# Split products for the shared experts, and four summed rows a token, in a 64-expert layer

## What is computed

```
logits = flat @ router_w.T
_, topk_idx = top_k(logits + router_bias, 4)
topk_w = softmax(logits)[topk_idx], divided by its sum
slot = number of the token among those of its expert (first 64 kept)
y = einsum(silu(xg @ gate_w) * (xg @ up_w), down_w)        (for each expert)
out = zeros.at[tok_table].add(y * w_table)
sg = einsum('nd,sfd->nsf', flat, sh_gate_w)                (s: 2 shared experts)
su = einsum('nd,sfd->nsf', flat, sh_up_w)
out = out + einsum('nsf,sdf->nd', silu(sg) * su, sh_down_w)
x = layernorm(x + out)
```

## Time and profile before

| | |
|---|---|
| time, median of 3 runs | 2373.93 us (2370.86 to 2379.55) |
| profiled execution | 2381.64 us |
| its span | 2379.9 us |
| PE busy, of the span | 2139.5 us (90%) |
| DVE, ACT, POOL busy | 1362.7, 806.4, 674.3 us |
| shared products in stage C (two recorded matmuls each) | 768 matmuls, 344.5 us busy |

### The profile page before, as it was taken

How to read it: one execution, slowest core, us unless ns; L and a number is a source line. 1 busy time by engine, 2 the same in 40 slices (tenths; PEclk the granted TensorE clock), 3 DMA queues, 4 the chain that set the end, 5 groups by cost and what they waited for, 6 DMA issues and landing times. The chain is left out here.

```text
span 2379.9 us, 31463 instructions
## 1 busy us (share of the span) xinstructions
PE 2139.5 (90%) x10918; PEld 1180.7 (50%) x10919; DVE 1362.7 (57%) x3185; ACT 806.4 (34%) x1333; POOL 674.3 (28%) x945
## 2 busy tenths in 40 slices
PE   9999979979999999879999988578888888889994
PEld 5777748755444443445555543233333333336763
DVE  5866768846121226566777774845656565445443
ACT  5554624420112211333444433533322232123333
POOL 1200015516433321223343433011113131214553
PEclk9999989979999999998999997789999999999997
DMA  7211232270177764363333330200000000065555
GB/s 268 75 36 54 89 121 82 94 290 1 28 240 248 244 210 152 100 134 81 81 88 82 88 68 1 97 3 1 2 19 2 19 28 19 19 177 159 100 99 171
DMA packets 101178, 230.31 MB, mean 97 GB/s; under 512 B 18886, under 2 KB 42626, under 8 KB 93870
## 3 DMA queue, kind: packets, MB, share of 16 engines
q1 hardware_dynamic: 78478, 186.61, 25.3%
q0 software_dynamic: 22560, 41.87, 7.9%
HBM read 169.45 MB, written 63.53 MB: 98 GB/s over the span
## 5 line engine op out<-in xcount | busy, mean ns | idle before, releaser
L2137 DVE CUSTOM_DVE_ANT_0 D_ps<-D_ps,D_mask 128x256 f32<-128x256 f32 (+1 forms) x512 | 186.6, 419 | 61.9 <-PE D_ps L2033 60.6
L1859 POOL TENSOR_SCALAR_AFFINE_SELECT D_probs<-D_probs 128x256 f32<-128x256 f32 x256 | 106.4, 422 | 288.2 <-ACT D_probs L1917 288.1
L1917 ACT ACTIVATE D_probs<-D_ps 128x512 f32<-128x512 f32 (+1 forms) x256 | 125.4, 543 | 184.4 <-PE D_ps L2055 184.3
L3170 DVE TENSOR_REDUCE F_neg_max<-F_ps 128x4 f32<-128x2048 f32 (+1 forms) x64 | 93.9, 1488 | 107.3 <-PE F_ps L3068 101.2
L2920 ACT ACTIVATE F_probs<-F_ps 128x1536 f32<-128x1536 f32 (+1 forms) x48 | 76.4, 1591 | 186.9 <-PE F_ps L3084 186.9
L1393 PE MATMUL C_ps<-C_down_shared,C_hs 128*128 128x512 f32 x256 | 114.0, 594 | 2.5 <-DVE C_hs L1560 1.5
L1381 PE MATMUL C_ps<-C_xT,C_gate_shared 128*128 128x512 f32 x256 | 115.4, 593 | 0.5 <-ACT C_xT L1256 0.5
L1381 PE MATMUL C_ps<-C_xT,C_up_shared 128*128 128x512 f32 x256 | 115.1, 592 | 0.0
L2033 PE MATMUL D_ps<-D_k_stack,D_q_stack 96*128 96x256 bf16 (+1 forms) x512 | 94.2, 270 | 15.2 <-DVE D_maxima L2137 11.8
L1230 POOL DMA_INDIRECT expert_sums<-C_y,C_of_slot x32 | 50.2, 1570 | 173.0 <-ACT C_y L1297 107.9
L2801 POOL TENSOR_SCALAR_AFFINE_SELECT F_probs<-F_probs 128x512 f32<-128x512 f32 x64 | 41.1, 654 | 180.5 <-ACT F_probs L2920 180.5
(11 more groups left out here) (574 smaller groups left out, 4947.7 us busy)
## 6 DMA issues: line engine op xcount, KB each, us to landing
C_ring<-moe_experts_dram SPq DMA_DIRECT2D x32, 1536.0 KB, 7.0
qk_parts<-D_parts SPq DMA_DIRECT2D x32, 384.0 KB, 2.6
expert_sums<-A_zeros SPq DMA_DIRECT2D x1, 8192.0 KB, 27.5
C_ring<-expert_sums SPq DMA_DIRECT2D x5, 1536.0 KB, 9.9
D_q_stack<-qk_parts SPq DMA_DIRECT2D x16, 384.0 KB, 4.7
D_k_stack<-qk_parts SPq DMA_DIRECT2D x16, 384.0 KB, 7.7
B_w<-ctxT_dram SPq DMA_DIRECT2D x1, 4096.0 KB, 16.8
B_c<-ctx_dram SPq DMA_DIRECT2D x4, 1024.0 KB, 8.2
```

What stands on the lines that cost most here:

```text
L1859: last = nc.gpsimd.affine_select(now[:, :, 0:P], now[:, :, 0:P], [[0, 2], [1, P]], ALU.is_ge, 0.0, base=0, channel_multiplier=-1)
L1917: nc.scalar.activation(probs[at % 2][:, 2 * pair:2 * pair + 2, 0:w], ps[:, 4 + unit % 3, :].rearrange("p (h q) -> p h q", h=2)[:, :, 0:w], ...
L2137: last = nc.vector.tensor_tensor_reduce(now, now, mask[:, first:256], 1.0, -3e38, ALU.add, ALU.max, maxima[n % 2][:, head, t:t + 1])
L3170: last = nc.vector.tensor_reduce(neg_max[n % 2][:, :, t], ps[:, 0:GROUP, at:at + w], AX_X, ALU.max, negate=True)
```

## The change

The shared products take split operands. Each f32 operand is written as a high part (a copy rounded to the type fp32r, by ACT) and a low part (the rest, by DVE), and a product becomes three products of fp32r operands: high by high, high by low, low by high. This is done for x, for the weights and for the hidden. For room, only one shared expert's weights are held at a time: the units now go through four batches with the first expert, then four with the second; x is held for two batches, written to memory (`x_spill`) and brought back for the second half. Batches 2 and 3 are turned among the early steps, of which there are 24; the routing of these batches moves with them. The table `sums` holds four rows a token, so POOL's stores need not add or wait for each other, and DVE adds the four rows at the end, one tile of tokens at a time.

```diff
-                         zeros[:].unsqueeze(1).to_broadcast([P, 2 * TILES, D])).then_inc(zeroed, 16)
+                         zeros[:].unsqueeze(1).to_broadcast([P, K_C * TILES, D])).then_inc(zeroed, 16)
...
-EARLY_STEPS = 20
+EARLY_STEPS = 24
...
-    for n in range(EARLY_STEPS, LATE):
-        middle.setdefault((n - EARLY_STEPS) * PAIRS // (LATE - EARLY_STEPS), []).append(n)
+    HALF = STEPS // 2
+    for n in range(EARLY_STEPS, HALF):
+        middle.setdefault(n - EARLY_STEPS + (-1 if n < HALF - KF else 0), []).append(n)
+    for n in range(HALF, LATE):
+        middle.setdefault(8 + (n - HALF) * (PAIRS - 8) // (LATE - HALF), []).append(n)
+    SECOND_GATES, SECOND_DOWN = 6, 10
...
+        x_spill = nc.dram_tensor("x_spill", (B, 2, P, KD * S), F32).ap()
+        x_hi = [sb(f"x_hi{j}", [P, KD, S], F32R) for j in (0, 1)]
+        x_raw, x_lo = zip(*(sb_over(f"x_raw{j}", [P, KD, S], f"x_lo{j}", [P, KD, S], F32R) for j in (0, 1)))
+        w_hi = [sb(n, [P, KD, 512], F32R) for n in ("gate_hi", "up_hi", "down_hi")]
+        w_raw, w_lo = zip(*(sb_over(n + "_raw", [P, KD, 512], n + "_lo", [P, KD, 512], F32R) for n in ("gate", "up", "down")))
+        ring_all, homes = sb_over("ring", [P, RING, 2, 3 * 512], "homes", [P, HOMES, K_C, D])
+        ring = [ring_all[:, r] for r in range(RING)]
...
+            def load_weights(half, *parts):
+                for part in parts:
+                    if half:
+
+                        sp.wait_ge((gate_s, up_s, down_s)[part], B * KF)
+                        sp.wait_ge(w_lo_ready[part], 1)
+                    source = (d["moe_sh_gate"].rearrange("(k p) f -> p k f", p=P)[:, :, half * 512:half * 512 + 512],
+                              d["moe_sh_up"].rearrange("(k p) f -> p k f", p=P)[:, :, half * 512:half * 512 + 512],
+                              d["moe_sh_down"].rearrange("(k p) n -> p k n", p=P)[:, half * KF:half * KF + KF, :])[part]
+                    sp.dma_start(w_raw[part][:], source).then_inc(w_in[part], 16)
+
+            def spill_x(b):
+                sp.wait_ge(x_hi_ready, KD * (b + 1))
+                sp.dma_start(x_spill[b, 0], x_hi[b % 2][:].bitcast(F32).rearrange("p k n -> p (k n)")).then_inc(spilled[b % 2], 16)
+                sp.wait_ge(x_lo_ready, b + 1)
+                sp.dma_start(x_spill[b, 1], x_lo[b % 2].bitcast(F32).rearrange("p k n -> p (k n)")).then_inc(spilled[b % 2], 16)
+
+            def bring_x(g):
+                sp.wait_ge(up_s, (B + g - 1) * KF)
+                sp.wait_ge(spilled[g % 2], 2 * 32)
+                sp.dma_start(x_hi[g % 2][:].bitcast(F32).rearrange("p k n -> p (k n)"), x_spill[g, 0]).then_inc(x_back[g % 2], 16)
+                sp.dma_start(x_lo[g % 2].bitcast(F32).rearrange("p k n -> p (k n)"), x_spill[g, 1]).then_inc(x_back[g % 2], 16)
+
+            load_weights(0, 0, 1, 2)
...
+            for b in range(B):
+                spill_x(b)
             sp.wait_ge(scattered, 16 * K_C * TILES)
             sp.dma_start(of_slot[:].rearrange("p n o -> p (n o)"), slots.rearrange("(p n) o -> p (n o)", p=P)).then_inc(slots_in, 16)
+            bring_x(0)
...
+                if q == 6:
+                    load_weights(1, 0, 1)
+                    bring_x(1)
+                if q == 11:
+                    load_weights(1, 2)
+                if q == 16:
+                    bring_x(2)
+                if q == 28:
+                    bring_x(3)
...
+            for t in range(TILES):
+                if t >= HOMES:
+
+                    sp.wait_ge(summed, t - HOMES + 1)
+                sp.dma_start(homes[:, t % HOMES].rearrange("p c n -> p (c n)"),
+                             sums.rearrange("(t p c) d -> p t (c d)", p=P, c=K_C)[:, t, :]).then_inc(sums_in[t % HOMES], 16)
...
-                if q >= 1:
-
-                    pool.wait_ge(stored[(q - 1) % 2], 16 * ((q - 1) // 2 + 1))
                 pool.indirect_dma_start(sums, bass.IndirectOffsetOnAxis(ap=of_slot[:, q, 1:2], axis=0), y[q % 2][:], None,
-                                        bounds_check=last_sum, oob_is_err=False, compute_op=ALU.add).then_inc(stored[q % 2], 16)
+                                        bounds_check=last_sum, oob_is_err=False).then_inc(stored[q % 2], 16)
...
+            def keep_x(b):
+                if b >= 2:
+
+                    act.wait_ge(up_s, (b - 1) * KF)
+                    act.wait_ge(spilled[b % 2], 32)
                 for k in range(KD):
                     act.wait_ge(x_turned, b * KD + k + 1)
-                    nc.scalar.copy(xT[:, k, b * S:(b + 1) * S], ps[:, 4 + k % 2, :]).then_inc(xT_ready, 1)
+                    nc.scalar.copy(x_raw[b % 2][:, k, :], ps[:, 4 + k % 2, :]).then_inc(x_raw_ready, 1)
+                    nc.scalar.copy(x_hi[b % 2][:, k, :], ps[:, 4 + k % 2, :]).then_inc(x_hi_ready, 1)
+
+            def high_of_hidden(m):
+                act.wait_ge(hs_raw_ready, m + 1)
+                nc.scalar.copy(hs_hi[:, m % KF, :], hs_raw[:, m % KF, :]).then_inc(hs_hi_ready, 1)
...
+                            nc.tensor.matmul(ps[:, bank + part, :], w_hi[part][:, k, now], x_hi[j][:, k, :], start=(k == 0), stop=False)
+                        if not half:
+                            pe.wait_ge(x_lo_ready, g + 1)
+                        for k in range(KD):
+                            nc.tensor.matmul(ps[:, bank + part, :], w_hi[part][:, k, now], x_lo[j][:, k, :], start=False, stop=False)
+                        pe.wait_ge(w_lo_ready[part], half + 1)
+                        for k in range(KD):
+                            last = nc.tensor.matmul(ps[:, bank + part, :], w_lo[part][:, k, now], x_hi[j][:, k, :], start=False,
+                                                    stop=(k == KD - 1))
...
-            turn_batch(2)
-            turn_batch(3)
             pe.wait_ge(converted, 1)
             places(0)
             for n in range(EARLY_STEPS):
                 shared_step(n)
                 if n == 1:
                     places(1)
-                if n == 2:
+                if n == 4:
+                    turn_batch(2)
+                if n == 6:
                     logits(2)
-                if n == 5:
+                if n == 10:
                     places(2)
-                if n == 7:
+                if n == 12:
+                    turn_batch(3)
+                if n == 14:
                     logits(3)
-                if n == 9:
+                if n == 18:
                     places(3)
...
+            def low_x(b):
+                dve.wait_ge(x_hi_ready, KD * (b + 1))
+                dve.wait_ge(logits_ready, b + 1)
+                nc.vector.tensor_tensor(x_lo[b % 2], x_raw[b % 2][:], x_hi[b % 2][:].bitcast(F32), ALU.subtract).then_inc(x_lo_ready, 1)
+
+            def low_of_weights(half, *parts):
+                for part in parts:
+                    dve.wait_ge(w_hi_ready[part], half + 1)
+                    nc.vector.tensor_tensor(w_lo[part], w_raw[part][:], w_hi[part][:].bitcast(F32), ALU.subtract).then_inc(w_lo_ready[part], 1)
+
+            def low_of_hidden(m):
+                dve.wait_ge(hs_hi_ready, m + 1)
+                nc.vector.tensor_tensor(hs_lo[:, m % KF, :], hs_raw[:, m % KF, :], hs_hi[:, m % KF, :].bitcast(F32), ALU.subtract
+                                        ).then_inc(hs_lo_ready, 1)
+
             def shared_step(n):
                 unit, down, i = step_of(n)
+                if i or down:
+                    if not down or i == 0:
+                        low_of_hidden(unit * KF + (KF if down else i) - 1)
...
-                if t % 3 == 0:
-                    dve.wait_ge(sums_in[t // 3 % RING], 16 * (t // 3 // RING + 1))
-                steps.after(nc.vector.tensor_tensor(acc[:, t, :], acc[:, t, :], sums_of(t, 0), ALU.add))
-                nc.vector.tensor_tensor(acc[:, t, :], acc[:, t, :], sums_of(t, 1), ALU.add).then_inc(summed, 1)
+                dve.wait_ge(sums_in[t % HOMES], 16 * (t // HOMES + 1))
+                steps.after(nc.vector.tensor_tensor(homes[:, t % HOMES, 0:2, :], homes[:, t % HOMES, 0:2, :], homes[:, t % HOMES, 2:4, :],
+                                                    ALU.add))
+                steps.after(nc.vector.tensor_tensor(acc[:, t, :], acc[:, t, :], homes[:, t % HOMES, 0, :], ALU.add))
+                nc.vector.tensor_tensor(acc[:, t, :], acc[:, t, :], homes[:, t % HOMES, 1, :], ALU.add).then_inc(summed, 1)
...
             pick(0)
             choose(0)
+            low_x(0)
             pick(1)
+            low_of_weights(0, 0, 1)
             share_out(0)
             shared_step(0)
             choose(1)
             shared_step(1)
             share_out(1)
+            low_of_weights(0, 2)
             shared_step(2)
...
+            low_x(1)
+            for n in range(3, EARLY_STEPS):
                 shared_step(n)
+                if n == 8:
+                    pick(2)
+                    low_x(2)
+                if n == 9:
+                    choose(2)
+                if n == 11:
```

(18 more changed lines are left out.)

157 lines of the change are left out of this document (79 added, 78 removed).

## The result

The changed kernel takes 2431.48 us (median of 4 runs, 2423.71 to 2434.97) where the kernel before takes 2375.30 in the same comparison (median of 4, 2370.86 to 2379.55): a ratio of 1.0232, 95% interval 1.0201 to 1.0264. It is 56 us slower. The forecast was 2406, 31 us slower; the time lies 1.5 us above its range of 2380 to 2430.

A forecast was written before the change was run, and what follows sets the result against it. TensorE (PE) was taken to bound stage C. First pair +45, pairs -37, transfers +8, clock +6 and end +10 made +32 us: 2406 us against the median, range 2380 to 2430.

The forecast's parts named there:

- The first pair: Stage C up to the first transpose of gathered rows: DVE's queue delays it from 636 to 681, +45 us.
- The pairs: The 32 pairs of stage C: PE work falls by 37 us, new transfers cost 8 us.
- -37 us; this term is the firmest: Shared steps among the 32 pairs: cheaper split products cut their PE work from 138 to 100 us.
- +8 us for this stall and what x for units 6 and 7 adds: Pairs: PE waits for ring loads queued behind new weight and x transfers; 8 us, bounds 0 and 15.
- The stall at pair 6: Pair 6's ring load needs 21 us with the transfers ahead of it, while PE arrives in 14 us.
- longer DMA: Rival, chance 0.20: short stretches of pairs without a shared step stall too, some 2 us at ten, +20: 2426.
- The end: Last two units to stage D: DVE's longer tiles hold PE up, 91 us becomes 101, +10; bounds -15 and +14.
- The clock: Stage C: new PE gaps at four places lower the granted clock, +6 us; bounds 0 and 15.
- The pace: Stage C products: a split product costs 0.232 us as in stage A, three 0.695, against 0.860 for f32.
- The prediction's other price: Stage C products: by the skill's four-pass rule three split products take 0.645 us; forecast would be 2399.
- The zeros in stage A: Stage A: twice the zeros, 27.5 us more transfer, free unless stage A's loads were late by 10 us.

The follow-up runs named there:

- e1: Changed kernel without its new transfers among the pairs: second-half weights and x not brought back, so that half computes from wrong data; 2408.3 us.
- e4: Changed kernel with the routing of batches 2 and 3 put earlier in the PE, DVE and ACT queues, no work added or removed; 2403.2 us.
- e7: Changed kernel with one transfer moved: x for unit 5 asked for ahead of the ring load of pair 13 instead of pair 6; 2426.7 us.
- e5: Changed kernel with the earlier routing of e4, 28 early steps, and second-half gate/up weights and unit 5's x requested ahead of pair 4's ring load; 2401.3 us.
- e8: e5 with three instead of two shared units behind the pairs, one tile of sums a step, later x requests; 2396.2 us, ratio to before 1.0096.
- e2: Changed kernel with the memory rows as before: two rows a token, stores that add and wait for the one ahead; 2428.6 us.

## Why the prediction was wrong, point by point

**The first pair: right.** +45 forecast, +46.4 measured (47.8 with the stage's later start). DVE's row of work came out as forecast where it counts: the last hidden ahead of share_out(3) at 642 (641.82 to 642.51 in the trace), its end at 650 (649.87), a wait of the third pass of a down behind share_out (7 forecast, 5.2 twice), PE idle about 20 us (22.4). The exact 642 is partly luck: the hidden of step 3 ended at 549.2, not 552 (DVE's row began 1.4 us earlier and was 1.1 shorter), and the stretch from there took 3 us longer than forecast. The chain behind share_out(3) was 33.8 us instead of 30.8: the gather took 6.2 us from issue to PE, not 3.5, because x for unit 4, which the prediction counted among the pairs, goes out ahead of it (e1). e4 shows the mechanism.

**The pairs: this step failed.** "-37 us; this term is the firmest" and "+8 us for this stall and what x for units 6 and 7 adds" make -29; measured -4.6. PE's work was nearly right: 223.0 us busy in e1, where the sum left 223 for the whole stretch with the 3 us that PE was idle before. Two things were not. The transfers cost 21.8 us (e1), not 8. The stall at pair 6, for which the prediction worked out 21 - 14 = 7, was 10.3. But x for units 6 and 7, for which the term leaves 1 us, cost 5.2 and 4.7 at the two ring loads behind it; 3.2 more follow at pair 20, and 4 us of slow clock. And without any of the new transfers the pairs still take 11 us more than PE's work (e1), for which the sum had no term. Together that is the miss of 24 us.

The sum compared 213 us of transfers with some 223 of time, called that fitting "on average", and then priced one place. What counted was how soon a load must land. A ring load can go out only when the pair four before is done, and e1 shows no wait at the three places when nothing long stands ahead; with 2.1 MB of x ahead the loads landed 15 to 16 us after their issue, and PE stood. e7 and e5 show it the other way: what is moved away takes its wait with it, and x for units 6 and 7, left in place, keeps its waits. The rival of "longer DMA", with 0.20, had the direction and nearly the time (2426), but partly by luck: it set 2 us at each of ten pairs without a shared step, and 20 of the 24 us stood at three loads. Waits of its kind are in e1, 4.2 us in all, and in e8.

**The end: right in mechanism, 3 us short.** +10 forecast, +13.3 measured. A tile takes 3.73 us (3.7), DVE is busy 79 of 105 us (75%, where the forecast said over 80), from 950.5 to 1022 with gaps of 1.3 us in all, and PE waits for it, through ACT's copy, 8.9 and 8.0 us. The sums are loaded 3.9 us into the end. e2 shows that the rows make it. What the prediction did not see is that they also pay in the pairs: it said that stores without add gain nothing before the end; e2 has them worth 10 us there, once PE is faster. So beside split products the rows cost 14.7 - 10.2 = 4.5 us net, not 10.

**The clock: not checked as a whole.** +6 forecast, of which "some 3 us lost" behind a gap stands in no row; 4 us stand in the pairs by e1, and lie inside the -4.6. The granted clock also fell from 1.00 to 0.86 ahead of the pairs and from 0.98 to 0.84 in the end, and no run separates what that cost there from PE's waits. **The pace: right.** 0.227 us a product (four in 0.907), so 0.68 for three, against 0.695. The prediction's other price, 0.645 for three, by which the forecast would have been 2399, is further off.

**The zeros in stage A: free, as taken.** Stage C's first transpose came 1.4 us later (488.15), within what the eleven traces differ by (486.26 to 488.70).

The pairs alone miss by 24 us, as much as the whole does; what the first pair (+1.4), the later start (+1.4) and the end (+3.3) miss by, the +6 for the clock makes up, since the clock's loss is already inside the measured stretches. The range ended at 2430 because it took the stall at 15 us at most, which would have left the pairs 22 us shorter than before; they were 4.6 shorter.

## What to carry to other kernels

Where an engine is made faster, look at each load that it will need sooner, and at what stands ahead of that load in its queue. A mean over the stage hides it: here the DMA engines had time left (0.71 of it used), and three loads behind new transfers cost PE 20 us. An operation added to the queue of an engine that has room still costs what stands behind it in that queue: here earlier places for the routing were worth 25 us, and one more addition a tile 9 us in the end, with DVE busy 52% and 74% of the time. When a cheaper product needs operands that no longer fit in on-chip memory, bringing them in is part of the product's price: here 22 us of 37.
